# One of three stages: where the feed-forward weights are brought on chip

## The chip, the cores and the metric

The program runs on one core of a Trainium2 chip. The metric is the device time of one execution in microseconds (us). TensorE is called PE, VectorE DVE, ScalarE ACT, GpSimd POOL, and SyncE, which issues all the DMAs of this kernel, SP.

## What is computed

The reference, cut to what matters:

```python
x = x + attention(cond(x, lang, W1, b1, W2, b2, gamma, beta), Wq, Wk, Wv, Wf, bf)   # cond: adapter + layer norm
y = cond2(x, expert, fc1_w, fc1_b, fc2_w, fc2_b, experts_w, experts_b)
    # h = gelu(x @ fc1_w.T + fc1_b); 192 outputs by the shared fc2_w, 64 by the expert of the batch element
def ffn(y):                                   # every weight is ternary (-1, 0, 1) with a scale for each output
    h = silu(tlin(y, w1_w, w1_s)) * tlin(y, w2_w, w2_s)     # tlin(x, w, s) = (x @ w.T) * s
    h = gelu(tlin(h, h1_w, h1_s))
    h = gelu(tlin(h, h2_w, h2_s))
    return tlin(h, w3_w, w3_s)
out = x + ffn(y)                              # x: (16, 256, 256) float32, hidden width 1024
```

## The kernel before

The 16 batch elements of 256 tokens go through three stages, one after the other, with the results of each kept in scratch tensors in the chip's memory.

**Attention stage.** A software pipeline over the batch elements: in one iteration `b`, PE does the adapter and the projections of element `b + 2`, a first pass of scores for the row maxima of `b + 1`, the scores proper of `b`, and the output products of `b - 1`. Twelve of these iterations are a loop of six pairs. The row maxima of an element become two more rows of its queries: ACT writes them to `m_t` (L518) and SP moves them with four small DMAs into `q_t` (`move_maxima`, L249 to L256), for which the first `scores` of that element waits (L943).

**Conditional stage** (L1110 to L1136). A loop over 8 tiles of 512 tokens. In each tile PE makes 8 units of the first layer (L1120, from `tile_hi` and `tile_lo`, the high and low part of the tile's input), then the shared output (L1127), then the output with the expert's columns (L1134). ACT applies the gelu into one of two buffers of `g_raw` (L567), and DVE splits each into `g_hi` and `g_lo` (L772, L774). After the eight splits of a tile, DVE splits the input of the next tile (`split_x`, L716 and L718), ors an eighth of the feed-forward weights into `bits` (`or_bits`, L756) and adds the biases into `y` (L792, L795). In the last tile the order differs: `or_bits` stands ahead of the eight splits, since the bits must be reduced by the end of the stage (L783 to L787); from them a flag is made that says whether the feed-forward may use its weights in one rounded pass. PE reads it and branches (L1195).

For each tile SP loads two experts (L327, L328; each needs a register loaded from memory first), and the next tile's input `tile_in` (L336), then waits until `y` is ready and stores it (L351). The next tile's loads come behind that wait. In the last tile the load of `tile_in` is that of the first input of the feed-forward (L349). POOL makes the high and low part of the expert's weights (L470, L473).

**Feed-forward stage** (L1165 to L1193). Again 8 tiles; PE multiplies with `ffn_w` (L1157), which lies on chip as a whole: 22,528 columns of float32 in 128 partitions, 11.5 MB.

How `ffn_w` gets there: the weights are first copied from the input to a scratch tensor (`store_ffn`, L263), a sixteenth (1,408 columns, `SHARE`) with each batch element of the attention stage, and from there loaded on chip (`load_ffn`, L267), also a sixteenth each time, behind a wait for its copy. Both are issued by SP in the attention stage. `CHECK` is an eighth, 2,816 columns. All DMAs go through one hardware queue, in the order in which SP issues them.

Of the kernel before, what the change touches and what calls it, by code (L numbers as in the profile page):

```python
# [17 lines left out]
B, T, D = 16, 256, 256  # L18
# [32 lines left out]
SHARE = FFN_COLS // B  # L51
CHECK = FFN_COLS // TILES
# [15 lines left out]
def build(nc, x_t, x_tok, lang, expert, cond_w1, cond_w2, cond_vec, w_qv, w_k, w_f, b_f, ident_d, mask_d, key_row_d,  # L68
          fc1_w, fc1_b, fc2_w, fc2_b, exp_w, exp_b, ffn_d, ffn_s, out_t):
    ctx = ExitStack()  # L70
    with ctx:
# [29 lines left out]
        s = {}  # L101
# [118 lines left out]
        def settle(eng, name):  # L220


            eng.sem_inc(s[name], 1)

        @block.sync
        def _(sp):
# [36 lines left out]
            def store_ffn(b):  # L263
                cols = bass.ds(b * SHARE, SHARE)
                sp.dma_start(ffn_scratch[:, cols], ffn_d[:, cols]).then_inc(s["ffn_copied"], 16)

            def load_ffn(b):  # L267
                cols = bass.ds(b * SHARE, SHARE)
                sp.wait_ge(s["ffn_copied"], 16 * (b + 1))
                settle(sp, "sp_settled")  # L270
                sp.dma_start(ffn_w[:, cols].bitcast(F32), ffn_scratch[:, cols]).then_inc(s["ffn_loaded"], 16)


            load_front(0)
            sp.dma_start(ident[:, :], ident_d).then_inc(s["const_loaded"], 16)
# [10 lines left out]
            load_front(1)  # L286
            load_front(2)
            store_ffn(0)
            load_ffn(0)
            move_maxima(0, 0)  # L290
            load_front(3)
            store_ffn(1)
            load_ffn(1)
            move_maxima(1, 1)
            with sp.Fori(0, (B - 4) // 2) as pair:
                for step in (1, 2):
                    b = 2 * pair + step
                    store_ffn(b + 1)
                    load_front(b + 3)
                    load_ffn(b + 1)  # L300
                    store_x1(b - 1)
                    load_resid(b)
                    move_maxima(b + 1, 1 - step % 2)
            sp.wait_ge(s["x1_stored"], HEAD + 16 * BT)
            sp.dma_start(xa[:, :, :], x1_scratch[:, :, 0:TW]).then_inc(s["xa_loaded"], 16)
            for b in range(B - 3, B + 1):
                if b < B - 1:
                    store_ffn(b + 1)
                    load_ffn(b + 1)
                store_x1(b - 1)  # L310
                if b < B:
                    load_resid(b)
                if b < B - 1:
                    move_maxima(b + 1, (b + 1) % 2)
                if b == B - 2:
                    sp.wait_ge(s["fc1_split"], 1)
                    sp.dma_start(fc1_raw[:, :], fc1_w[:, 1]).then_inc(s["raw_loaded"], 16)
            sp.wait_ge(s["x1_stored"], HEAD + 16 * B)
            sp.wait_ge(s["phase1_over"], 4)


            sp.dma_start(fc2_raw[:, :, :], fc2_w).then_inc(s["fc2_loaded"], 16)
# [15 lines left out]
            def cond2_tile(t, more):  # L338
                if not is_first(t):
                    sp.wait_ge(s["expert_split"], HEAD + BT * t)  # L340
                    sp.wait_ge(s["y_ready"], HEAD + (1 + BT) * t)
                    settle(sp, "sp_settled")
                load_expert(t)
                if more:
                    load_x(t + 1)
                else:
                    sp.wait_ge(s["xa_split"], HEAD + TILES)
                    sp.wait_ge(s["y_stored"], HEAD + 16)
                    sp.dma_start(yc[:, :, :], y_scratch[:, :, 0:TW]).then_inc(s["yc_loaded"], 16)  # L349
                sp.wait_ge(s["y_ready"], HEAD + (1 + BT) * (t + 1))  # L350
                sp.dma_start(y_scratch[:, :, bass.ds(t * TW, TW)], y[:, :, :]).then_inc(s["y_stored"], 16)  # L351
# [238 lines left out]
        def _(dve):  # L590
# [148 lines left out]
            dve.wait_ge(s["phase1_over"], 4)  # L739


            dve.wait_ge(s["ffn_loaded"], 16 * B)
            def split_y(t):
                dve.wait_ge(s["yc_loaded"], 16 * (t + 1))
                if is_first(t):
# [6 lines left out]

            def or_bits(t):

                dve.wait_ge(s["bits_step"], t + 1)
                nc.vector.tensor_tensor(bits[:, :], bits[:, :], ffn_w[:, bass.ds(t * CHECK, CHECK)].bitcast(U32), ALU.bitwise_or).then_inc(s["bits_step"], 1)  # L756

# [508 lines left out]
```

## Time and profile before

| | |
|---|---|
| median of 3 runs | 1232.09 us (1232.05 to 1235.82) |
| the profiled execution | 1232.09 us, its span 1230.4 us |
| attention stage | 0 to about 387 us of the span |
| conditional stage | about 387 to 573 us |
| feed-forward stage | about 579 us to the end |
| PE busy | 1179.1 us, 96% of the span |
| DVE busy | 692.0 us, 56% |
| DMA | 18.6% of 16 engines' span, 70.44 MB |

PE is busy nearly throughout, so what matters is what PE does and where it stands still. The profiled execution took what the median run took, so sums against it are sums against the median.

### The profile page before, as it was taken

The page shows a single profiled execution, that of the slowest core. Times are in us where ns is not written, and L with a number is a line of the kernel's source. Part 1 is how long each engine was busy: PE and PEld are TensorE (multiplying, and loading weights), DVE is VectorE, ACT ScalarE, POOL GpSimd, SP SyncE. Part 2 cuts the span into 40 slices and gives each one's busy share as a digit, 9 for nine tenths or more (in the row PEclk, how much of TensorE's full clock was granted, in tenths as well). Part 3 has the DMA queues.
Part 4 walks back from the last instruction along what each step waited for, and adds up shares of the span by engine and source line. Part 5 has one row for each costly group of instructions (what it writes and reads, how often), then busy time and mean ns, then how long its engine had stood idle before and what let it go on. Part 6 is the DMA issues. An engine that isn't in the chain of part 4 may idle for free.

```text
span 1230.4 us, 19224 instructions
## 1 busy us (share of the span) xinstructions
PE 1179.1 (96%) x6404; PEld 942.4 (77%) x6434; DVE 692.0 (56%) x1264; ACT 400.4 (33%) x649; POOL 171.8 (14%) x235
## 2 busy tenths in 40 slices
PE   4899999999988899997999999999999999999998
PEld 3577777777756788886888888888888888888886
DVE  2867767676754887886535335335353263443532
ACT  1456465555643323222212213122122131221221
POOL 1233333334332211311000000000000000000000
PEclk9999999999999899998999999999999999999999
DMA  3343444444432212222001001010010010100100
GB/s 97 114 132 112 130 123 125 124 128 122 135 101 67 71 51 77 76 68 87 1 1 52 0 0 51 0 51 0 0 51 0 0 51 0 51 0 0 34 0 17
DMA packets 45417, 70.76 MB, mean 58 GB/s; under 512 B 12096, under 2 KB 26320, under 8 KB 45392
## 3 DMA queue, kind: packets, MB, share of 16 engines
q1 hardware_dynamic: 45392, 70.44, 18.6%
q8 instruction: 14, 0.23, 0.1%
q14 instruction: 11, 0.09, 0.0%
HBM read 57.32 MB, written 24.12 MB: 66 GB/s over the span
## 4 chain that ended last, share of the span: by engine, by line
PE 88%; DVE 6%; issue 2%; DMA 1%; SPq 1%; ACT 1%; POOL 1%; DVEq 0%; POOLq 0%; ACTq 0%
PE bank L1157 53%; PE bank L1120 6%; PE bank L1134 3%; PE bank L949 3%; PE bank L930 3%; PE bank L1127 3%; PE bank L970 2%; PE bank L1007 2%; DVE neg_max L640 2%; PE bank L912 2%; PE bank L896 2%; PE bank L933 1%; PE bank L885 1%; PE bank L870 1%; PE bank L862 1%
## 5 line engine op out<-in xcount | busy, mean ns | idle before, releaser
L1157 PE MATMUL bank<-h_lo,ffn_w 128*128 128x512 f32 x1152 | 450.8, 391 | 0.0
L1157 PE MATMUL bank<-h_hi,ffn_w 128*128 128x512 f32 x1152 | 450.8, 391 | 0.0
L1157 PEld LDWEIGHTS bank<-h_lo,ffn_w 128*128 128x128 f32 x1152 | 216.4, 188 | 47.3
L1157 PEld LDWEIGHTS bank<-h_hi,ffn_w 128*128 128x128 f32 x1152 | 216.3, 188 | 47.3
L819 DVE CAST h_hi<-h_raw 128x512 fp32r<-128x512 f32 x192 | 82.1, 427 | 300.3 <-ACT h_raw L587 298.1
L587 ACT ACTIVATE h_raw<-bank,scales 128x512 f32<-128x512 f32 x128 | 87.2, 687 | 322.0 <-PE bank L1157 321.9
L640 DVE TENSOR_REDUCE neg_max<-bank 128x2 f32<-128x512 f32 (+1 forms) x192 | 126.1, 686 | 53.0 <-remote 42.1
L821 DVE TENSOR_TENSOR h_lo<-h_raw,h_hi 128x512 fp32r<-128x512 f32 x192 | 133.0, 693 | 6.6
L501 ACT ACTIVATE p<-bank 128x512 f32<-128x512 f32 x192 | 111.3, 598 | 68.8 <-PE bank L949 65.2
L1157 PE MATMUL bank<-tile_hi,ffn_w 128*128 128x512 f32 x256 | 101.5, 397 | 7.0 <-issue 7.0
L1157 PE MATMUL bank<-tile_lo,ffn_w 128*128 128x512 f32 x256 | 101.3, 396 | 0.0
L949 PE MATMUL bank<-q_t,keys 128*128 128x512 f32 x192 | 94.8, 511 | 4.6 <-DMA q_t<-m_t 4.1
L930 PE MATMUL bank<-keys,q_t 128*128 128x256 f32 (+1 forms) x256 | 85.6, 390 | 7.3 <-DVE neg_max L640 6.4
L429 POOL TENSOR_SCALAR_AFFINE_SELECT p<-p 128x512 f32<-128x512 f32 (+1 forms) x96 | 75.7, 789 | 72.8 <-ACT p L501 72.8
L930 PEld LDWEIGHTS bank<-keys,q_t 128*128 128x128 f32 x256 | 47.8, 190 | 20.1 <-DVE neg_max L640 10.7
L829 DVE SCALAR_TENSOR_TENSOR h_raw<-bank,scales,sil 128x512 f32<-128x512 f32 x64 | 47.8, 746 | 27.0 <-ACT sil L580 27.0
L1157 PEld LDWEIGHTS bank<-tile_hi,ffn_w 128*128 128x128 f32 x256 | 48.9, 191 | 17.9 <-issue 7.1
L580 ACT ACTIVATE sil<-bank,scales 128x512 f32<-128x512 f32 x64 | 43.3, 688 | 55.7 <-PE bank L1157 54.4
L1157 PEld LDWEIGHTS bank<-tile_lo,ffn_w 128*128 128x128 f32 x256 | 48.8, 191 | 10.7
L774 DVE TENSOR_TENSOR g_lo<-g_raw,g_hi 128x512 fp32r<-128x512 f32 x64 | 54.4, 849 | 2.2
L567 ACT ACTIVATE g_raw<-bank,fc_bias 128x512 f32<-128x512 f32 x64 | 43.3, 690 | 34.8 <-DVE g_lo L774 17.9
L949 PEld LDWEIGHTS bank<-q_t,keys 128*128 128x128 f32 x192 | 37.6, 197 | 16.6 <-ACT p L501 7.8
(110 smaller groups left out, 1494.3 us busy)
## 6 DMA issues: line engine op xcount, KB each, us to landing
ffn_scratch<-in_ffn_d SPq DMA_DIRECT2D x16, 704.0 KB, 4.5
ffn_w<-ffn_scratch SPq DMA_DIRECT2D x16, 704.0 KB, 4.1
xt<-in_x_t SPq DMA_DIRECT2D x16, 256.0 KB
xtok<-in_x_tok SPq DMA_DIRECT2D x16, 256.0 KB
resid<-in_x_t SPq DMA_DIRECT2D x16, 256.0 KB, 3.1
x_scratch<-x SPq DMA_DIRECT2D x16, 256.0 KB, 2.6
tile_in<-x_scratch SPq DMA_DIRECT2D x8, 512.0 KB, 4.1
exp_raw<-in_exp_w SPq DMA_DIRECT2D x16, 256.0 KB, 2.7
```

The lines of the kernel that those rows point to most:

```text
L429: nc.gpsimd.affine_select(out=v, in_=v, compare_op=ALU.is_ge, fill=0.0, base=0, pattern=[[0, v.shape[1]], [1, P]], channel_multiplier=-1). ...
L501: nc.scalar.activation(dst.rearrange("p c t -> p (c t)"), score_bank[par][:, :], ACT.Exp).then_inc(s["exp_done"], 1)
L587: nc.scalar.activation(h_raw[:, m % 2, :], banks[g % 8][:, :], ACT.Gelu, scale=sc[:, m:m + 1]).then_inc(s["c_act"], 1)
L640: nc.vector.tensor_reduce(neg_max[:, t, first:first + pairs, :].rearrange("p c a -> p (c a)"), max_bank[u % 2][:, :].rearrange("p (c k) -> ...
L774: nc.vector.tensor_tensor(g_lo[:, m, :], g_raw[:, m % 2, :], g_hi[:, m, :].bitcast(F32), ALU.subtract).then_inc(s["act_ready"], 1)
L819: nc.vector.tensor_copy(dst_hi, src).then_inc(s["c_hi"], 1)
L821: nc.vector.tensor_tensor(dst_lo, src, dst_hi.bitcast(F32), ALU.subtract).then_inc(s["c_ready"], 1)
L829: nc.vector.scalar_tensor_tensor(out=h_raw[:, m % 2, :], in0=banks[(2 * m + 1) % 8][:, :], scalar=SC_W2[:, m:m + 1], in1=sil[:, m % 2, :], ...
L930: mm(dst[:, 2 * c * seen:2 * (c + 1) * seen].rearrange("p (a k) -> p a k", a=2), q_t[odd][:, first + c, t * P:(t + 1) * P], keys[odd][:, : ...
L949: mm(score_bank[par][:, :].rearrange("p (c t) -> p c t", c=pairs), keys[odd][:, par, k0:k0 + P], q_t[odd][:, first:first + pairs, q0:T], s ...
L1120: last = mm(banks[m % 6][:, :], w[:, k, cols], v[:, k, :], start=i == 0, stop=i == len(passes) - 1)
L1157: last = mm(bank, w_at(at, k, width, m), v_at(v, k), start=k == 0 and i == 0, stop=k == tiles - 1 and i == 1)
```

## The change

The load of the feed-forward weights is taken out of the attention stage, where it stood behind the wait for the copy. The copies stay. SP now issues one load of an eighth (1,408 KB instead of 704 KB) in each tile of the conditional stage, behind the two experts' loads and ahead of the load of `tile_in`. SP waits once, at the end of the attention stage, until all copies have landed. DVE, which waited at the beginning of the conditional stage for all 16 loads, now waits in each `or_bits(t)` for load `t`.

```diff
--- before.py
+++ after.py
@@ -264,12 +264,9 @@
                 cols = bass.ds(b * SHARE, SHARE)
                 sp.dma_start(ffn_scratch[:, cols], ffn_d[:, cols]).then_inc(s["ffn_copied"], 16)
 
-            def load_ffn(b):
-                cols = bass.ds(b * SHARE, SHARE)
-                sp.wait_ge(s["ffn_copied"], 16 * (b + 1))
-                settle(sp, "sp_settled")
+            def load_ffn(t):
+                cols = bass.ds(t * CHECK, CHECK)
                 sp.dma_start(ffn_w[:, cols].bitcast(F32), ffn_scratch[:, cols]).then_inc(s["ffn_loaded"], 16)
-
 
             load_front(0)
             sp.dma_start(ident[:, :], ident_d).then_inc(s["const_loaded"], 16)
@@ -286,18 +283,15 @@
             load_front(1)
             load_front(2)
             store_ffn(0)
-            load_ffn(0)
             move_maxima(0, 0)
             load_front(3)
             store_ffn(1)
-            load_ffn(1)
             move_maxima(1, 1)
             with sp.Fori(0, (B - 4) // 2) as pair:
                 for step in (1, 2):
                     b = 2 * pair + step
                     store_ffn(b + 1)
                     load_front(b + 3)
-                    load_ffn(b + 1)
                     store_x1(b - 1)
                     load_resid(b)
                     move_maxima(b + 1, 1 - step % 2)
@@ -306,7 +300,6 @@
             for b in range(B - 3, B + 1):
                 if b < B - 1:
                     store_ffn(b + 1)
-                    load_ffn(b + 1)
                 store_x1(b - 1)
                 if b < B:
                     load_resid(b)
@@ -317,6 +310,7 @@
                     sp.dma_start(fc1_raw[:, :], fc1_w[:, 1]).then_inc(s["raw_loaded"], 16)
             sp.wait_ge(s["x1_stored"], HEAD + 16 * B)
             sp.wait_ge(s["phase1_over"], 4)
+            sp.wait_ge(s["ffn_copied"], 16 * B)
 
 
             sp.dma_start(fc2_raw[:, :, :], fc2_w).then_inc(s["fc2_loaded"], 16)
@@ -341,6 +335,7 @@
                     sp.wait_ge(s["y_ready"], HEAD + (1 + BT) * t)
                     settle(sp, "sp_settled")
                 load_expert(t)
+                load_ffn(t)
                 if more:
                     load_x(t + 1)
                 else:
@@ -739,7 +734,6 @@
             dve.wait_ge(s["phase1_over"], 4)
 
 
-            dve.wait_ge(s["ffn_loaded"], 16 * B)
             def split_y(t):
                 dve.wait_ge(s["yc_loaded"], 16 * (t + 1))
                 if is_first(t):
@@ -752,6 +746,7 @@
 
             def or_bits(t):
 
+                dve.wait_ge(s["ffn_loaded"], 16 * (t + 1))
                 dve.wait_ge(s["bits_step"], t + 1)
                 nc.vector.tensor_tensor(bits[:, :], bits[:, :], ffn_w[:, bass.ds(t * CHECK, CHECK)].bitcast(U32), ALU.bitwise_or).then_inc(s["bits_step"], 1)
```

The order on SP around the first move of maxima (names are those of the tensors, destination first; ISA and REGISTER rows work out addresses). Before:

```order
L265 DMA ffn_scratch<-in_ffn_d 128x1408
L271 DMA ffn_w<-ffn_scratch 128x1408 [waits ffn_copied]
L256 DMA q_t<-m_t 1x8x256 [waits max_t_out]
L256 DMA q_t<-m_t 1x8x256 x3
L229 TENSOR_LOAD in_lang_ptr
```

With the change:

```order
L265 DMA ffn_scratch<-in_ffn_d 128x1408
L256 DMA q_t<-m_t 1x8x256 [waits max_t_out]
L256 DMA q_t<-m_t 1x8x256 x3
L229 TENSOR_LOAD in_lang_ptr
L229 REGISTER_ALU
```

The load and its wait no longer stand between the copy and the moves of maxima.

SP in a tile of the conditional stage, from the second expert on. Before:

```order
L327 DMA exp_raw<-in_exp_w 128x512
L328 ISA
L328 DMA fc_bias<-in_exp_b 64x1
L335 REGISTER_ALU
L336 ISA [waits xa_split]
L336 DMA tile_in<-x_scratch 128x2x512
L350 ISA
L351 ISA [waits y_ready]
L351 DMA y_scratch<-y 256x1x512
```

With the change:

```order
L321 DMA exp_raw<-in_exp_w 128x512
L322 ISA
L322 DMA fc_bias<-in_exp_b 64x1
L269 ISA
L269 DMA ffn_w<-ffn_scratch 128x2816
L329 REGISTER_ALU
L330 ISA [waits xa_split]
L330 DMA tile_in<-x_scratch 128x2x512
L345 ISA
L346 ISA [waits y_ready]
L346 DMA y_scratch<-y 256x1x512
```

The load of an eighth stands in front of the load of the next tile's input.

DVE at the beginning of the last tile. Before:

```order
L806 COMPARE_AND_BRANCH
L756 TENSOR_TENSOR bits<-bits,ffn_w 128x2816 [waits bits_step]
L772 CAST g_hi<-g_raw 128x512 [waits raw_ready]
L774 TENSOR_TENSOR g_lo<-g_raw,g_hi 128x512 [waits hi_ready]
L772 CAST g_hi<-g_raw 128x512 [waits raw_ready]
```

With the change:

```order
L801 COMPARE_AND_BRANCH
L751 TENSOR_TENSOR bits<-bits,ffn_w 128x2816 [waits bits_step,ffn_loaded]
L767 CAST g_hi<-g_raw 128x512 [waits raw_ready]
L769 TENSOR_TENSOR g_lo<-g_raw,g_hi 128x512 [waits hi_ready]
L767 CAST g_hi<-g_raw 128x512 [waits raw_ready]
```

The order is the same; the `or_bits` in front of the splits now also waits for a load.

## Rows read from the trace of the kernel before

**Rows 1.** Windows: length, busy us of PE PEld DVE ACT POOL, clock, DMA share, GB/s

```profile
231.60:253.10 21.50, 21.12 (x166) 15.70 (x167) 15.62 (x38) 12.10 (x23) 8.08 (x12) 1.00 0.42 126
316.00:338.00 22.00, 21.62 (x168) 15.98 (x169) 16.19 (x38) 12.31 (x24) 8.08 (x12) 1.00 0.52 160
528.00:550.00 22.00, 22.00 (x121) 19.18 (x120) 17.53 (x23) 6.70 (x9) 4.95 (x4) 1.00 0.23 72
```

**Rows 2.** Chain of work that ended last, conditional stage: start us, us, what

```profile
538.74 5.44 PE bank L1127 x24
544.18 5.75 PE bank L1134 x48
549.94 9.56 PE bank L1120 x42
...
573.40 5.80 issue
```

**Rows 3.** Timeline, 41 to 48 us: start us, us, engine, line, work [idle before <-releaser]

```profile
41.99 0.37 ACT L518 ACTIVATE m_t<-bank 32x256 fp32r<-32x256 f32 x1 [4.87 <-PE bank L938]
...
42.82 0.36 SPq L271 DMA_DIRECT2D ffn_w<-ffn_scratch  x1
...
43.29 2.88 SPq L256 DMA_DIRECT2D q_t<-m_t  x4
...
47.77 0.50 PE L949 MATMUL bank<-q_t,keys 128*128 128x512 f32 x1 [1.36 <-DMA q_t<-m_t]
```

**Rows 4.** Timeline of SP, seventh and last tile of the conditional stage

```profile
536.74 0.59 SPq L336 DMA_DIRECT2D tile_in<-x_scratch  x1
551.01 0.65 SPq L351 DMA_DIRECT2D y_scratch<-y  x1
...
558.09 0.61 SPq L349 DMA_DIRECT2D tile_in<-y_scratch  x1
```

**Rows 5.** DMA issues: form, count, KB each, median us from issue to landing

```profile
ffn_w<-ffn_scratch SPq DMA_DIRECT2D x16, 704.0 KB, 4.1
...
tile_in<-x_scratch SPq DMA_DIRECT2D x8, 512.0 KB, 4.1
```

**Rows 6.** The line of the load, L271: spread of its landings

```profile
DMA to landing us min/median/max: 3.9/4.1/5.3
```

**Rows 7.** Windows, the first microseconds of the feed-forward stage

```profile
578.00:580.00 2.00, 0.80 (x2) 0.72 (x3) 0.00 (x0) 0.00 (x0) 0.00 (x0) 0.50 0.43 116
580.00:582.00 2.00, 2.00 (x6) 1.51 (x6) 0.00 (x0) 0.63 (x1) 0.00 (x0) 0.50 1.01 354
```

**Rows 8.** Timeline of DVE, end of the seventh tile

```profile
542.03 1.77 DVE L716 CAST tile_hi<-tile_in 128x1024 fp32r<-128x1024 f32 x1
...
547.98 0.75 DVE L792 TENSOR_SCALAR y<-bank,fc_bias 128x512 f32<-128x512 f32 x1
549.97 0.88 DVE L795 TENSOR_SCALAR y<-bank,fc_bias 128x256 f32<-128x256 f32 x2 [1.24 <-PE bank L1134]
```

**Rows 9.** Timeline of DVE, last tile

```profile
550.77 3.08 DVE L756 TENSOR_TENSOR bits<-bits,ffn_w 128x2816 uint32<-128x2816 uint32 x1
553.77 0.42 DVE L772 CAST g_hi<-g_raw 128x512 fp32r<-128x512 f32 x1
554.22 0.69 DVE L774 TENSOR_TENSOR g_lo<-g_raw,g_hi 128x512 fp32r<-128x512 f32 x1
...
559.09 0.42 DVE L772 CAST g_hi<-g_raw 128x512 fp32r<-128x512 f32 x1
...
563.47 1.66 DVE L774 TENSOR_TENSOR g_lo<-g_raw,g_hi 128x512 fp32r<-128x512 f32 x1
565.05 0.68 DVE L749 CAST tile_hi<-tile_in 128x1024 fp32r<-128x1024 f32 x1
...
572.47 0.86 DVE L795 TENSOR_SCALAR y<-bank,fc_bias 128x256 f32<-128x256 f32 x2
```

**Rows 10.** Timeline of POOL, last tile

```profile
561.54 3.04 POOL L473 TENSOR_TENSOR fc2b_lo<-exp_raw,fc2b_hi 128x512 fp32r<-128x512 f32 x2
```

## The prediction

> **What bounds the kernel now.** I read the windows of the stages first, to see where PE has time to give back. In the attention stage PE is busy 21.12 of 21.50 us of one iteration, and 21.62 of 22.00 in a stretch with more DMA traffic: in both 0.38 us idle at full clock. In a tile of the conditional stage it is busy 22.00 of 22.00 us [rows 1]. So in the loops of both stages PE is the limit, and a transfer matters only where PE or its feeder waits for it. Then the chain of waits: it runs along PE through the tiles, but behind the last first-layer units (549.94 + 9.56 = 559.50) it leaves PE and runs along DVE up to 573.4, where 5.8 us follow in which the stages change over [rows 2]. DVE in the last tile is busy without a hole from 550.77 to 573.3 [rows 9]. That is the place to watch: what delays DVE there delays the end by the same amount. Last, the timelines of SP and DVE, for who issues a load when, and who needs it.
>
> **Part 1: the load and its wait leave the attention stage.** In the loop nothing waits for them: the 0.38 us are PE's own. I take 0. The bound on the gain is that all idle goes, 0.38 x 13 iterations = 4.9 us; since a stretch at 160 GB/s has the same idle time as one at 126 [rows 1], I stay at 0.
>
> At the first move of maxima there is a gain. SP waits there for the copy, issues the load at 42.82 and the moves from 43.29 on; but ACT has `m_t` ready at 41.99 + 0.37 = 42.36 [rows 3]. Without the load the moves go out at about 42.4, 0.9 us earlier. PE had waited 1.36 us for them at 47.77 [rows 3], so it can use all of it: **-0.9** (bounds 0, if another engine is late next, and -1.4, PE's whole wait). What is late next is PE's own work before, which ends at 47.77 - 1.36 = 46.4.
>
> At the stage's end SP waits for the last copy, which was issued with element 15 some 40 us before: 0.
>
> **Part 2: seven tiles of the conditional stage.** The load of an eighth takes the place in SP's order of the load of `tile_in`, which was issued at 536.74 and landed 4.1 us later, at 540.8; DVE came to it at 542.03 [rows 4, 5, 8]. The queue works the loads off in order, so the landing of `tile_in` moves back. A sixteenth (704 KB) lands in 4.1 us [rows 5]. The rate of the fullest stretch is 354 GB/s [rows 7]; another 704 KB at it are 2.04 us, so the eighth lands 6.1 us after its issue, and the 512 KB of `tile_in` behind it take 1.48 us more: 7.6, at 544.3.
>
> What can the chain bear? From DVE's start on `tile_in` to its first `y` are 547.98 - 542.03 = 5.95 us, in which the cast took 1.77 us; undisturbed it takes 0.68 [rows 8, 9], so 4.86 us. The second `y` waits for PE until 549.97, and the first takes 0.75 [rows 8]. So `tile_in` may land at 549.97 - 0.75 - 4.86 = 544.4 at the latest. My estimate is 544.3: **it just fits, term 0**. PE itself needs the split only at 549.94 [rows 2] and has slack (544.3 + 1.9). But SP issues the next tile's loads only when `y` is ready. So beyond 544.4, each tenth is paid again in each of the six tiles before the last: the chain load, split, `or_bits`, `y` would be the limit and not PE. Bounds: the landing lies between 542.9 (the eighth and `tile_in` move side by side: 4.1 + 2.04) and 545.5 (the slowest landing of a sixteenth, 5.3 [rows 6], + 2.04 + 1.48). Above 544.4 that is 1.1 us a tile: 0 to +6.6.
>
> The Trainium skill, "DMA: Bandwidth & Descriptors", section on the anatomy of one DMA, fits a transfer as 2.0 us plus its bytes at 436 GB/s; by that, an estimate, eighth and `tile_in` together land after 6.5 us instead of 7.6, and the fit would leave a spare of about a microsecond. The same page's bandwidth section gives about 358 GB/s for memory-side transfers, and our 354 agrees [rows 7].
>
> **Part 3: the last tile.** Here `or_bits` stands ahead of the splits, and the eighth it needs is issued only after SP has stored the `y` of the tile before (551.01) and fetched two experts: at 558.09, where the load of `tile_in` stood [rows 4]. It lands at 558.1 + 6.1 = 564.2. DVE would have begun at 550.77 [rows 9] and now stands for 13.4 us, with all eight splits and everything to the stage's end queued behind. Not all of it is lost. Before, the splits took 565.05 - 553.77 = 11.28 us, since the last ones were slowed (1.66 us against 0.69) [rows 9] while POOL worked on the experts' weights up to 564.6 [rows 10]. Now POOL is done before they begin, and they run at the pitch of the first ones, (559.09 - 553.77) / 5 = 1.064 us, so 8.5 us [rows 9]. `or_bits` from 564.2, splits from 567.2 (3.0 us as before, 550.77 to 553.77), done at 575.7 instead of 565.05: **+10.6**. From there DVE's way to the second `y` is 7.4 us as before (565.05 to 572.47), so it starts at 583.1.
>
> Does PE cover or add anything? It has finished its first-layer units (they need only two gelus, which no split holds up) and stands from 560.7 to 568. Its shared output follows the splits (5.44 / 8 = 0.68 us for each against a pitch of 1.06), ends at 576.4, and the experts' output ends 5.75 us later [rows 2], at 582.2, 0.9 before DVE wants it. Nothing is added at full clock.
>
> Bounds: the eighth lands like a sixteenth (4.1) and the term is 8.6; it takes 5.3 + 2.04 = 7.3 and the term is 11.9; if in addition the splits run as slowly as before, 14.7.
>
> **Sum.** -0.9 + 0 + 10.6 = +9.7 on the profiled execution of 1232.1 us, which is also the median: **1241.8 us**.
>
> **Rivals.**
>
> *A. The tiles become bound by the loads.* Same mechanism as in part 2, with a landing past 544.4. At 1.1 us in each of six tiles the time is 1241.8 + 6.6 = 1248.4; half of that, 1245.1, is as likely. For it: my estimate leaves 0.1 us. Against: DVE and SP had nothing that late before. Chance 0.22.
>
> *B. A cold PE in the last tile.* PE stands for over 7 us there. After the pause of at least 5.8 us at the stage's end [rows 2] the granted clock was 0.50 when it came back [rows 7], that is 1.2 instead of 2.4 GHz. At half clock all through, the experts' output takes 11.5 us, ends at 587.9, and the end is 4.8 later: 1246.6. Against it: PE has 8 us of fairly dense work between, which should bring the clock back before. The Trainium skill, "TensorE: Matmul & The Clock Gate", section on HAM oscillation, names pauses for a DMA between bursts as what sends the clock down, and counts the time at half clock as half lost; if only the shared output is hit, nothing is lost here, since DVE sets its pace. Chance 0.06.
>
> *C. The attention loop gives back its idle time* (4.9 us): 1236.9. The same idle at different traffic [rows 1] speaks against it. Chance 0.05.
>
> *D. The traffic slows the engines in the attention stage,* not by waits but in the instructions themselves, and without 704 KB of writes in each iteration they run shorter. From 9.7 / 13 = 0.75 us in an iteration of 21.5 this decides, and at 1.1 us (5%) the time is 1241.8 - 14.3 = 1227.5, faster. Against it: two iterations whose traffic differs by a quarter have the same PE time. The Trainium skill, "SBUF — State Buffer", section on the bandwidth pool, says contention there is a matter of locked ports and not of a shared total, which excludes D. Chance 0.03.
>
> *E. The wait is shorter than I think,* for instance since SP reaches the eighth earlier. For no measurable change (within 0.3%, 3.7 us, about what a measurement of this kernel can tell) it must land before 558.2, when by its rows it is just being issued [rows 4]. Chance 0.03.
>
> **How the numbers follow.** The forecast has 0.61. Its own bounds are 1239.3 (parts at -1.4, 0, 8.6) to 1244.0 (0, 0, 11.9). The range takes it in with most of A and B: 1239.0 to 1249.0, leaving out C, D, E and the far end of A. Slower by over 0.3%: forecast, A, B and most of C, 0.92. Within: E and a rest of C, 0.05. Faster: D, 0.03.
>
> **What the new profile would show.** The chain of waits should have a DMA of `ffn_w` in the last tile, and DVE's `or_bits` there a wait of some 13 us that such a landing ended, with the first split at about 566 (all 0.9 earlier than above). PE should be idle some 7 us behind its last first-layer units. POOL should be done before the splits, and these be even at 1.06 us. PE in the middle tiles should stay at 22.0 of 22.0 us with a pitch of 22.1; a pitch of 22.5 or more, with DVE waiting for `tile_in`, is rival A. Iterations of the attention stage should keep their 21.5 us, and the first scores come 0.9 us earlier. I am wrong in kind if DVE does not wait in the last tile, or if the attention iterations get shorter by more than 0.3 us.

## The result and the profile after

| | before | with the change |
|---|---|---|
| median (20 runs each) | 1234.58 us (1230.87 to 1249.10) | 1244.83 us (1242.13 to 1257.58) |
| the profiled execution | 1232.09 us | 1247.21 us |
| its span | 1230.4 us | 1245.5 us |
| first scores / first store of `y` / last store of `y` | 47.77 / 418.30 / 573.36 | 46.56 / 418.99 / 588.20 |

The time is 1.0075 times that of before, with an interval of 1.0053 to 1.0097, that is 6.5 to 12.0 us more. The forecast was 1241.8 us and +9.7. The profiled executions lie 2.5 us below the median of their kernel (before) and 2.4 above it (after), so their spans, 15.1 us apart, show too much. Where they differ for another reason than the change is said below. Three of the 20 executions before and one of the 20 after took 13 to 15 us more than the median of the rest; without these four the medians are 1233.70 and 1244.73 us, 11.0 apart.

The page of the changed kernel: the engines' busy time, and their shares of the chain that ended last.

```profile
PE 1185.8 (95%) x6404; PEld 945.8 (76%) x6434; DVE 675.7 (54%) x1264; ACT 400.6 (32%) x649; POOL 169.0 (14%) x235
...
PE 75%; DVE 9%; DMA 5%; SPq 5%; issue 4%; ACT 1%; POOL 0%; DVEq 0%; POOLq 0%; ACTq 0%
```

A PE busy for 95% of the span still looks like the only limit. But DMA and SP's queue hold a tenth of the chain. Where they enter it, the chain shows (rows from the seventh tile on; start us, us, what):

```profile
540.24 0.43 SPq L269
540.97 6.95 DMA tile_in<-x_scratch
548.03 0.70 DVE tile_hi L711
...
549.90 2.52 DVE bits L751
...
554.61 0.66 SPq L346
...
561.65 6.70 DMA ffn_w<-ffn_scratch
568.38 3.09 DVE bits L751
571.47 0.35 DVE g_hi L767
...
586.64 0.75 DVE y L787
...
588.24 5.80 issue
594.04 16.05 PE bank L1152 x59
```

Before, this stretch ran along PE up to 559.50 and then along DVE [rows 2]. Now it goes round through the loads. The landing of `tile_in` releases DVE's split, `or_bits` and `y` follow, then SP's store, and behind the store the next loads. In the last tile the link is the landing of the eighth.

DVE at the same two places (start us, us, engine, line, work, idle before and what ended it):

```profile
548.03 0.69 DVE L711 CAST tile_hi<-tile_in 128x1024 fp32r<-128x1024 f32 x1 [5.42 <-DMA tile_in<-x_scratch]
...
568.38 3.09 DVE L751 TENSOR_TENSOR bits<-bits,ffn_w 128x2816 uint32<-128x2816 uint32 x1 [13.94 <-DMA ffn_w<-ffn_scratch]
571.39 0.42 DVE L767 CAST g_hi<-g_raw 128x512 fp32r<-128x512 f32 x1
571.84 0.69 DVE L769 TENSOR_TENSOR g_lo<-g_raw,g_hi 128x512 fp32r<-128x512 f32 x1
...
579.89 0.69 DVE L743 CAST tile_hi<-tile_in 128x1024 fp32r<-128x1024 f32 x1
```

The wait of 13.94 us answers to an `or_bits` that began without one at 550.77 [rows 9]. The eight splits behind it take 579.89 - 571.39 = 8.50 us. They took 11.28 when POOL's work lay beside them [rows 9, 10].

SP in the seventh and the last tile (start us, us, engine, line, work), against [rows 4]:

```profile
540.24 0.43 SPq L269 DMA_DIRECT2D ffn_w<-ffn_scratch  x1
540.97 0.60 SPq L330 DMA_DIRECT2D tile_in<-x_scratch  x1
554.61 0.66 SPq L346 DMA_DIRECT2D y_scratch<-y  x1
...
561.65 0.59 SPq L269 DMA_DIRECT2D ffn_w<-ffn_scratch  x1
```

The landings (form, count, KB each, median us from issue to landing), against 4.1 us for 704 KB and 4.1 us for 512 KB in [rows 5]:

```profile
ffn_w<-ffn_scratch SPq DMA_DIRECT2D x8, 1408.0 KB, 6.4
...
tile_in<-x_scratch SPq DMA_DIRECT2D x8, 512.0 KB, 7.0
```

At the start, two pieces of the chain and PE's first scores, against 43.29 and the 1.36 us of [rows 3]:

```profile
42.37 0.79 SPq L256
...
44.59 1.93 DMA q_t<-m_t
...
46.56 0.50 PE L944 MATMUL bank<-q_t,keys 128*128 128x512 f32 x1 [0.24 <-DMA q_t<-m_t]
```

**Where the time went, by stretches of the profiled executions.** The eight stores of `y` cut the conditional stage into pieces that don't depend on a choice of mine.

| stretch | before | after | difference |
|---|---|---|---|
| to the first scores | 47.77 | 46.56 | -1.21 |
| from there to the first store of `y` | 370.53 | 372.43 | +1.90 |
| six tiles, first to seventh store | 132.71 | 135.62 | +2.91 |
| last tile, seventh to eighth store | 22.35 | 33.59 | +11.24 |
| last store to the end of the span | 657.0 | 657.3 | +0.3 |

Through nearly all of the attention stage the second row stays near zero: from the second to the 14th element the changed kernel begins its scores 1.17 to 1.30 us earlier. With the 15th the lead falls to 0.49 us, and with the 16th it is 0.95. The 1.90 us are lost at that stage's end and in the first tile. There the granted clock is at its lower level, 1.2 GHz, for different lengths in different executions. Windows on PE of the kernel before (length, PE busy, clock, DMA share, GB/s):

```profile
360.00:370.00 10.00, 6.18 (x74) 0.93 0.34 109
370.00:380.00 10.00, 8.73 (x91) 0.90 0.16 47
403.00:418.00 15.00, 12.13 (x63) 0.77 0.00 0
```

and with the change:

```profile
360.00:370.00 10.00, 6.46 (x74) 0.84 0.36 108
370.00:380.00 10.00, 9.24 (x88) 0.82 0.16 49
403.00:418.00 15.00, 11.70 (x59) 0.77 0.21 81
```

The experiments suggest that this is chance and not the change. Ten executions were profiled in which the early move of maxima has no load ahead of it. Their first store of `y` came at 415.81 to 419.30, mean 417.96. Four with the load ahead of it: 418.30 to 420.55, mean 419.12. The means differ by 1.2 us, the size of the gain at the first scores. But the ten alone spread over 3.5 us, so the two means don't prove it.

### The profile page after: what moved, and what is told of

Its sections match the earlier page's. It is cut to its first block, busy times and chain, and to the rows that moved or that the text cites. A ratio compares the mean times of both kernels' runs of the same rounds, so it can differ in the third digit from the quotient of the medians.

```text
span 1245.5 us, 19192 instructions
## 1 busy us (share of the span) xinstructions
PE 1185.8 (95%) x6404; PEld 945.8 (76%) x6434; DVE 675.7 (54%) x1264; ACT 400.6 (32%) x649; POOL 169.0 (14%) x235
## 4 chain that ended last, share of the span: by engine, by line
PE 75%; DVE 9%; DMA 5%; SPq 5%; issue 4%; ACT 1%; POOL 0%; DVEq 0%; POOLq 0%; ACTq 0%
PE bank L1152 52%; PE bank L944 3%; DMA tile_in<-x_scratch 3%; PE bank L925 3%; PE bank L1002 2%; DVE neg_max L635 2%; PE bank L965 2%; PE bank L907 2%; SPq L320 2%; PE bank L891 2%; DVE bits L751 1%; PE bank L928 1%; PE bank L880 1%; PE bank L865 1%; PE bank L857 1%
## 5 line engine op out<-in xcount | busy, mean ns | idle before, releaser
L1152 PEld LDWEIGHTS bank<-tile_lo,ffn_w 128*128 128x128 f32 x256 | 48.9, 191 | 10.8
L944 PEld LDWEIGHTS bank<-q_t,keys 128*128 128x128 f32 x192 | 38.0, 199 | 15.9 <-ACT p L496 7.9
L928 PE MATMUL bank<-mask,ident_b 128*128 128x256 bf16 (+1 forms) x162 | 49.5, 305 | 0.0
```

The lines of the kernel that those rows point to most:

```text
L928: mm(diag, ident_b[:, :], mask[:, 0:2 * pairs, :], start=False, stop=True).then_inc(s["max_mm"], 1)
L944: mm(score_bank[par][:, :].rearrange("p (c t) -> p c t", c=pairs), keys[odd][:, par, k0:k0 + P], q_t[odd][:, first:first + pairs, q0:T], s ...
L1152: last = mm(bank, w_at(at, k, width, m), v_at(v, k), start=k == 0 and i == 0, stop=k == tiles - 1 and i == 1)
```

## The experiments

The runs came in three sets of four, in the order in which they stand here. Each set has its own runs of the kernel before: medians 1233.92, 1234.23 and 1233.48 us. Every ratio is against those of its set. Line numbers in rows are those of each kernel. Diffs are against the changed kernel unless they say otherwise.

**One tile early.** In tile `t` the eighth of tile `t + 1` is loaded, and eighth 0 at the end of the attention stage.

```diff
+                    sp.wait_ge(s["ffn_copied"], 32)
+                    load_ffn(0)
             sp.wait_ge(s["x1_stored"], HEAD + 16 * B)
...
                 load_expert(t)
-                load_ffn(t)
                 if more:
+                    load_ffn(t + 1)
                     load_x(t + 1)
```

> The changed kernel, but each eighth is loaded one tile earlier (the first at the end of the attention stage), so the last tile issues no load. Theory (the last tile's wait costs most, the lateness of tile_in the rest): the wait of 13.9 us on DVE in the last tile goes and the last tile is 11.2 us shorter, while the middle tiles stay at a pitch of 22.6 us: about 1244.8 - 11.2 = 1233.6. Rival (the middle tiles are most of the loss, the wait is mostly covered): the last tile gets less than 4 us shorter and the time stays over 1240.

Measured: 1234.47 us, ratio 1.0011 (0.9975 to 1.0047). The last tile takes 22.34 us as before, and no wait for `ffn_w` is left: the loss is in the last tile's wait. My expectation for the middle tiles missed. Their pitch is (552.00 - 419.23) / 6 = 22.13 us, though DVE still waits 3.48 us for `tile_in` in the seventh. The landing is just early enough here. Yet `tile_in` stands behind a whole eighth as with the change. From the issue of the eighth both had landed after 7.34 to 7.41 us in five of the six tiles, where the change needed 7.72 to 8.24. Why the same two loads land sooner here stays open.

**The input first.** `tile_in` goes ahead of the eighth of the same tile.

```diff
                 load_expert(t)
-                load_ffn(t)
                 if more:
                     load_x(t + 1)
...
+                load_ffn(t)
                 sp.wait_ge(s["y_ready"], HEAD + (1 + BT) * (t + 1))
```

> The changed kernel, but SP issues the load of tile_in ahead of the eighth. Theory: tile_in lands some 4 us after its issue again, the middle tiles go back to a pitch of 22.1 us (six tiles, -3.1 us), and the last eighth lands 1.5 us later, since the 512 KB are in front of it: about 1244.8 - 3.1 + 1.5 = 1243.2. Rival (the middle tiles are late because of the wait for the eighth in or_bits, not because of tile_in): the pitch stays at 22.6 and the time rises to about 1246.

Measured: 1245.53 us, ratio 1.0109 (1.0063 to 1.0155). The pitch of the middle tiles is back at (548.72 - 415.81) / 6 = 22.15, so it was the place behind the eighth that made `tile_in` late. The last tile pays: `or_bits` waits 15.28 us and the tile takes 34.95. By the profiles that is some 2.7 us gained and 1.4 lost; the timing can't tell this kernel from the changed one.

**Both.** `tile_in` first, then the eighth of the next tile; eighth 0 at the end of the attention stage, as in the one-tile-early run.

```diff
                 load_expert(t)
-                load_ffn(t)
                 if more:
                     load_x(t + 1)
+                    load_ffn(t + 1)
```

> One tile early and behind tile_in. Theory: both losses go, and the 1.2 us that the first move of maxima gained stay: about 1234.6 - 1.2 = 1233.4, pitch 22.1 us, no wait in the last tile. Rival (the loads in the conditional stage cost by their traffic, wherever they stand): 1237 or more.

Measured: 1231.43 us, ratio 0.9977 (0.9944 to 1.0011). Its windows hold no loss: pitch (550.64 - 417.57) / 6 = 22.18, last tile 22.33, first scores at 46.65. Its chain runs from tile to tile along PE alone, as in [rows 2]:

```profile
499.96 5.16 PE bank L1131 x43
505.12 10.91 PE bank L1117 x48
516.03 5.44 PE bank L1124 x24
521.47 5.86 PE bank L1131 x48
527.33 10.91 PE bank L1117 x48
```

It has seven of the change's eight loads in the conditional stage (eighth 0 is issued at 364.8), and its ratio is 0.9977 where the change has 1.0075, some 12 us less. Against the kernel before it is 2.5 us faster by the medians, but the interval holds 1.

**The check behind the splits.** The last tile's `or_bits` moves behind the splits and behind `split_y`.

```diff
             def cond2_tile(t, more):
-                if not more:
-                    or_bits(t)
                 for m in range(KH):
...
                     split_y(0)
+                    or_bits(t)
```

> The changed kernel, but in the last tile the or of the last eighth stands behind the eight splits and the split of the next input, so the splits do not queue behind the wait. Theory: the eighth lands at 568.3 in the profile of the changed kernel, the splits end at about 567.5 and the split of the input at 569.4, so DVE never stands for the load; the second y starts about 9 us earlier: about 1235.5. Rival (what costs is the landing itself, whatever stands behind it): the time stays within 3 us of 1244.8.

Measured: 1239.70 us, ratio 1.0056 (1.0023 to 1.0089). The wait for the eighth is gone and the last tile falls from 33.59 to 26.56 us, but not to the value expected. DVE in that tile:

```profile
564.96 0.98 DVE L767 TENSOR_TENSOR g_lo<-g_raw,g_hi 128x512 fp32r<-128x512 f32 x1
570.16 0.69 DVE L743 CAST tile_hi<-tile_in 128x1024 fp32r<-128x1024 f32 x1 [4.22 <-DMA tile_in<-y_scratch]
```

The expected 1235.5 missed: I had overlooked that the feed-forward's first input is queued behind the same eighth. Once `or_bits` no longer hides it, its landing is the next wait, 4.22 us.

**The changed kernel again.** No edit.

> The changed kernel once more, for a second profile. Theory: the pitch of the middle tiles is again 22.4 us or more and DVE waits there for tile_in, DVE waits about 13.5 us in the last tile; which stretches run at half clock differs. Rival (the 22.6 us of the first profile were a chance of that execution): pitch 22.2 or less.

Measured: 1246.09 us, ratio 1.0121 (1.0077 to 1.0165). The profile repeats the pieces: pitch (552.93 - 416.82) / 6 = 22.69, last tile 33.19 with a wait of 13.53, and first scores at 46.60.

**Half the bytes.** A sixteenth of each pair is loaded in the attention stage behind its copy, as before, and the other in its tile.

```diff
             def load_ffn(t):
-                cols = bass.ds(t * CHECK, CHECK)
+                cols = bass.ds(t * CHECK + SHARE, SHARE)
...
             store_ffn(0)
+            load_half(0)
             move_maxima(0, 0)
```

> The changed kernel, but half of each eighth (a sixteenth, 704 KB) is loaded in the attention stage behind its copy, as before the change, and the other half in the tile. Theory (the bytes in front of tile_in and of the last check cost): tile_in lands some 2.3 us earlier than with the eighth, so the middle tiles are bound by PE again at 22.1 us (-3), and the wait in the last tile shrinks by 2.3 us; the 1.2 us at the first move of maxima are gone again. About 1244.8 - 3 - 2.3 + 1.2 = 1240.7. If SP's register loads are late in the loop by some 0.35 us also here, that lateness comes from the added instructions in the loop and not from the bytes.

Measured: 1244.34 us, ratio 1.0108 (1.0057 to 1.0160). Of the pieces, these went about as expected: the pitch is (553.24 - 420.55) / 6 = 22.12, the last wait is 12.11 us, 1.83 less than 13.94 where 2.3 was expected, and the first scores are back at 47.94. The first store of `y` came 1.6 us later than with the change, and the last tile, 32.41, is only 1.2 shorter, since its `or_bits` took 3.73 us instead of 3.09. Its profile alone would give 1243.3 - 1245.5 = -2.2 us of span, where the medians show -0.5, and -1.8 against the 1246.09 of the changed kernel in the same set. The expected 1240.7 missed. Halving the bytes removes a small part of the loss, at a size that these six runs can't tell from none.

**Twice the bytes.** Each tile loads two eighths, of which the second is the next tile's; weights are so loaded twice.

```diff
+                cols = bass.ds(0 if isinstance(t, int) else (t + 1) * CHECK, CHECK)
+                sp.dma_start(ffn_w[:, cols].bitcast(F32), ffn_scratch[:, cols]).then_inc(s["ffn_loaded"], 16)
...
-                dve.wait_ge(s["ffn_loaded"], 16 * (t + 1))
+                dve.wait_ge(s["ffn_loaded"], 32 * (t + 1))
```

> The changed kernel, but each tile loads two eighths (the second again in its own tile, the last time the first eighth), and each or waits for both. 1408 KB more in front of tile_in. Theory: tile_in lands 1441792 bytes / 354 GB/s = 4.1 us later plus 0.4 us of issue, which the chain of load, split, or and y passes on in full: pitch about 22.6 + 4.5 = 27.1 us in six tiles, and 4.5 us more in the last: about 1244.8 + 31.5 = 1276. Rival (PE is the limit of the middle tiles and the load is covered): pitch under 23 and the time about 1250.

Measured: 1269.33 us, ratio 1.0279 (1.0247 to 1.0311), less than the 1276 expected. The pitch is (574.22 - 419.30) / 6 = 25.82, 3.2 us over that of the change, and the last wait 16.70. So the tiles of this kernel are bound by the loads, as rival A has it, and each further microsecond of landing is paid in each tile. DVE in the sixth tile:

```profile
541.72 0.69 DVE L713 CAST tile_hi<-tile_in 128x1024 fp32r<-128x1024 f32 x1 [10.58 <-DMA tile_in<-x_scratch]
542.44 1.23 DVE L715 TENSOR_TENSOR tile_lo<-tile_in,tile_hi 128x1024 fp32r<-128x1024 f32 x1
543.59 3.08 DVE L753 TENSOR_TENSOR bits<-bits,ffn_w 128x2816 uint32<-128x2816 uint32 x1
```

The split begins 19.2 us after the store of `y` (522.49), and with the change 15.9 in the seventh tile (548.03 - 532.13); the means over six tiles are 19.3 and 16.0. The second eighth cost 3.3 us and not the 4.1 that 354 GB/s [rows 7] give: 1,408 KB in 3.3 us are 437 GB/s. A window (length, busy us of PE PEld DVE ACT POOL, clock, DMA share, GB/s) shows it directly:

```profile
534.00:538.00 4.00, 2.62 (x20) 2.19 (x19) 0.00 (x0) 0.00 (x0) 1.91 (x2) 1.00 1.04 439
```

**The last eighth first.** In the last tile the eighth goes ahead of the two experts.

```diff
+                if not more:
+                    load_ffn(t)
                 load_expert(t)
                 if more:
+                    load_ffn(t)
                     load_x(t + 1)
```

> The changed kernel, but in the last tile SP issues the eighth ahead of the two experts. Theory: it is issued about 0.7 us behind the store of y instead of 7.0, so the wait in the last tile ends some 6.3 us earlier; POOL's work on the experts falls into the splits again and costs up to 2.8 us of that: 1244.8 - 6.3 + (0 to 2.8), about 1240. Rival (SP's issue isn't what makes the eighth late): less than 2 us gained.

Measured: 1243.03 us, ratio 1.0077 (1.0050 to 1.0105); that is 3.1 us less than the changed kernel in the same set, where 3.5 to 6.3 were expected. The eighth is issued 0.97 us after the store of `y` instead of 7.04, and the wait falls by 5.4 us. Half of that is lost again (last tile 30.89 us, 2.7 less), since now the experts come late and POOL's work lies beside the splits once more. DVE in that tile:

```profile
560.21 3.09 DVE L753 TENSOR_TENSOR bits<-bits,ffn_w 128x2816 uint32<-128x2816 uint32 x1 [8.51 <-DMA ffn_w<-ffn_scratch]
...
564.99 1.50 DVE L769 CAST g_hi<-g_raw 128x512 fp32r<-128x512 f32 x1
566.52 1.63 DVE L771 TENSOR_TENSOR g_lo<-g_raw,g_hi 128x512 fp32r<-128x512 f32 x1
```

The splits take 574.45 - 563.22 = 11.2 us here, against 8.5 with the change. That is the saving which part 3 of the prediction had counted, with its sign turned.

**The kernel before again.** No edit to the kernel before.

> The kernel before once more, for a second profile and for what two timings of one kernel differ by. The sum of the changed kernel's parts against the first profile of before (13.5 to 15.1 us) is larger than the difference of the medians (10.3 and 11.9). If the first profile was a lucky one, PE's places in this one are 1 to 3 us later by the end, above all at the stage changes, where stretches at half clock differ; if not, they agree within 0.5 us and the rest of the gap stays open. Ratio to before: 1.000.

Measured: 1234.76 us, ratio 1.0022 (0.9993 to 1.0052). Two timings of one kernel thus differ by 0.2%, 2.7 us. Its pitch and last tile are 22.1 and 22.34 us, as in the first profile. Its first scores come at 48.48, 0.7 us later than there, after a wait of 2.15 us for the same moves, and its last store of `y` at 573.89, 0.5 us later. So the gain at the first scores is 1.2 to 1.9 us, by which profile of before it is measured.

**The moves first.** Against the kernel before: the first move of maxima goes ahead of the first load.

```diff
             store_ffn(0)
-            load_ffn(0)
             move_maxima(0, 0)
+            load_ffn(0)
```

> The kernel before with one change: SP issues the four moves of the first maxima ahead of the first load of weights and its wait. Theory: all of the change's gain in the attention stage is this place: the first scores come 1.1 to 1.2 us earlier and stay so through the twelve iterations, time 1.1 us less or lost in the spread. Rival (the gain needs the loads gone from the loop): PE is back at its old places within the loop.

Measured: 1231.61 us, ratio 0.9988 (0.9966 to 1.0011). PE:

```profile
46.54 0.50 PE L949 MATMUL bank<-q_t,keys 128*128 128x512 f32 x1 [0.24 <-DMA q_t<-m_t]
```

The first scores come at 46.54, as with the change. So the gain at the start is one of order, and is to be had without moving any load out of the stage. That it reaches the end of the program agrees with the medians, but the interval holds 1.

**A small load in the tile.** Against the kernel before: everything stays, and SP loads 4 columns (2 KB) in each tile at the place of the eighth, for which `or_bits` waits. SP also waits once for all 16 loads before the conditional stage.

```diff
                 load_expert(t)
+                cols = bass.ds(t * CHECK, 4)
+                sp.dma_start(ffn_w[:, cols].bitcast(F32), ffn_scratch[:, cols]).then_inc(s["bit_loaded"], 16)
...
+                dve.wait_ge(s["bit_loaded"], 16 * (t + 1))
                 dve.wait_ge(s["bits_step"], t + 1)
```

> The kernel before with one more DMA of 2 KB (four columns of ffn_w, again) in each tile of the conditional stage, where the changed kernel has its eighth, and a wait for it in the or of the tile. It tells apart why SP issues the first expert's load 3.5 to 4.0 us behind the store of y in the loop instead of 3.2 to 3.4. If the added instructions in the loop do it, it is at 3.6 also here; if the bytes in flight, at 3.3. Time as before, ratio within 0.002, pitch 22.1 us: 2 KB don't delay tile_in.

Measured: 1243.01 us, ratio 1.0074 (1.0042 to 1.0106), where a ratio within 0.002 was expected. I had meant it to price the instructions alone and had not thought of the last tile. It is the clearest run of the study. SP issues the load there 7.55 us after the store of `y`; it lands 1.9 us later, and DVE stands:

```profile
560.78 3.16 DVE L760 TENSOR_TENSOR bits<-bits,ffn_w 128x2816 uint32<-128x2816 uint32 x1 [9.64 <-DMA ffn_w<-ffn_scratch]
563.86 0.83 DVE L776 CAST g_hi<-g_raw 128x512 fp32r<-128x512 f32 x1
564.73 1.63 DVE L778 TENSOR_TENSOR g_lo<-g_raw,g_hi 128x512 fp32r<-128x512 f32 x1
```

The last tile takes 31.81 us, 9.5 more than before, for 2 KB. Of the change's wait of 13.94 us, some 9.6 are the place in SP's order, with the 1.9 us in which even 2 KB land, and some 4.3 are the bytes. The split is rough, since SP issued the load 0.5 us later here than with the change. The middle tiles stay at (551.30 - 418.67) / 6 = 22.1.

**Input, experts, next eighth.** A try at something better still, with eighth 0 at the end of the attention stage as before.

```diff
-                load_expert(t)
-                load_ffn(t)
                 if more:
                     load_x(t + 1)
+                load_expert(t)
+                if more:
+                    load_ffn(t + 1)
```

> As the kernel with both repairs (one tile early, behind tile_in), but SP issues tile_in ahead of the experts too, so that it lands long before DVE wants it. Theory: the pitch is 22.1 in all middle tiles (instead of 22.1 to 22.2), the last tile has no wait, the start gain of 1.1 us stays: about 1231 against 1234.3. The experts come 0.8 us later; POOL is done some 0.8 us later, and PE wants them only behind the shared output. Rival: POOL's later work falls on other DVE instructions and gives back up to 1 us a tile.

Measured: 1261.11 us, ratio 1.0222 (1.0171 to 1.0273), where about 1231 was expected: a plain miss. Its six runs lie between 1250.80 and 1268.79 us, and the profiled one, 1251.50, is near the lowest. So what the profile shows explains about 18 us of the loss, and what made the other runs longer stays open. The first expert's load is issued 5.6 us after the store of `y` (424.37 - 418.73) instead of 3.6. POOL starts later and lies beside DVE's tile split and `or_bits`. POOL in two tiles:

```profile
433.27 5.20 POOL L471 TENSOR_TENSOR fc2b_lo<-exp_raw,fc2b_hi 128x512 fp32r<-128x512 f32 x2
...
460.46 6.21 POOL L471 TENSOR_TENSOR fc2b_lo<-exp_raw,fc2b_hi 128x512 fp32r<-128x512 f32 x2
```

against 3.04 us in [rows 10]. PE's waits (total us, times, longest):

```profile
PE bank L1132 <- POOL fc2b_lo L471: 14.1, 6, 4.5
```

PE stops in six tiles. Behind the first two stops its granted clock also falls: 0.84 and 0.87 in the windows 435 to 440 and 440 to 447, 0.57 and 0.79 in 465 to 470 and 470 to 476. The stores of `y` are 28.3, 29.3 and then 23.6 to 23.8 us apart; the last tile has its 22.3.

## Why the prediction was right, and where not

**The attention stage, term -0.9: right, measured -1.2.** The moves went out at 42.37 instead of 43.29, 0.9 us earlier as said. The other 0.3 us the term didn't have: the last move landed 1.93 us after its issue (44.59 to 46.52), and before, with the load ahead of it in the queue, 2.19 us (45.53 to 47.72). PE's wait shrank from 1.36 to 0.24 us, and nothing else took its place. The moves-first run gives the same with the load kept, so it was the load's place ahead of the moves. In the profile of after this gain is hidden by the 1.90 us of clock and stage end; the ten-against-four comparison agrees with it, without proving it. Rivals C and D are out: the gap between the kernels is -1.17 to -1.30 us through the whole loop, so its iterations kept their length with 704 KB of writes fewer in each. The Trainium skill, "SBUF — State Buffer", in its section on the bandwidth pool, says that transfers and engines don't share a total; the trace agrees.

**The middle tiles, term 0: this step failed.** The text said "it just fits", with a landing at 544.3 against a limit of 544.4. Its terms added up without rounding give 544.36 for both, so the sum had no spare at all, and the 0.1 us counted against rival A was rounding. Counted from the store of `y`, the limit was 544.4 - 528.92 = 15.5 us; measured were 15.9 in the seventh tile. Two sizes were off in that tile. SP issued the eighth 8.1 us after the store (540.24 - 532.13) where `tile_in` had been at 7.8 (536.74 - 528.92): the first expert's load is already later by that. And the two landings together took 7.8 us (548.03 - 540.24) where I had 7.6. That is rival A at half of its size, since the pitch rose by 0.48 us (after) and 0.57 (again) and not by 1.1: +2.9 and +3.4 us. The size varies: two more kernels keep the change's order in these tiles, and there the pitch was (555.04 - 419.26) / 6 = 22.63 in the check-behind run, but only (551.87 - 417.70) / 6 = 22.36 in the last-eighth-first run, +3.1 and +1.5 us. PE's windows hardly betray it (22.25 of 22.50 us busy in the seventh tile), since PE's next first-layer units had slack: they begin at 552.17 in the last tile, 2.2 us after 549.94 [rows 2], while the store of `y` slipped by 3.6 (554.61 - 551.01). What counts is the store, for the last eighth is queued behind it. The input-first, both and half-the-bytes runs each take the landing back under the limit, and the pitch with it; twice the bytes raises it by 3.2.

Why SP's first load of a tile comes 0.3 to 0.4 us later in kernels with an eighth in the loop stays open. The small load adds the same instruction, and there that load is issued 3.2 to 3.4 us after the store as before and the middle tiles kept their 22.1 us, so it is not the instruction alone. Nor is it bound to an eighth: in the second profile of before one tile in six has it at 3.65, and with half the bytes two in six at 3.7.

**The last tile, term +10.6: right, measured +11.2 and +10.8.** All links are in the rows. The eighth was issued 7.04 us after the store of `y` (estimate 7.08), and took 6.7 us where I had 6.1. The splits then ran at 1.06 us each as said, since POOL was done. PE stood 9.4 us and not the 7 of the text: the store of `y`, behind which the eighth is queued, had slipped 1.4 us further than PE's own work, and the landing took 0.6 longer.

```profile
572.68 0.77 PE L1122 MATMUL bank<-g_hi,fc2a_hi 128*128 128x512 f32 x1 [9.44 <-DVE g_lo L769]
```

The landing is the term's error. The Trainium skill, "DMA: Bandwidth & Descriptors", section on the anatomy of one DMA, has 2.0 us and 436 GB/s, an estimate of 5.3 us for an eighth. It gives this fit for DMAs that GpSimd issues, which the prediction didn't say; all loads here are SP's, and the median landing was 6.4. For 2 KB, though, its fixed part fits the 1.9 us seen here, and its rate fits the 437 GB/s of a second eighth.

Rival B, the cold PE, came and cost nothing. The clock was at the lower level for most of 568 to 579 us:

```profile
568.00:579.00 11.00, 6.32 (x16) 0.53 0.04 17
579.00:588.00 9.00, 8.00 (x60) 1.00 0.00 0
```

There PE follows DVE's splits. At 1.2 GHz it needs 1.28 us for the three products of a split (573.24 to 574.52, and again to 575.80), and the splits come every 1.06 us, so it fell behind, but only by a little. It was back at 2.4 GHz for the experts' output, which began at 580.97 and, at 5.75 us as before [rows 2], ended at 586.7, 0.6 before DVE wanted it at 587.31. Rival E would have needed the landing at 558.2; it came at 568.4.

**The sum.** By the profiles the parts are -1.2, +2.9 to +3.4 and +10.8 to +11.2, together +13. The medians say +10.3 (+9.3 by the ratio, 6.5 to 12.0) and, in the second timing, +11.9 (+14.9 by the ratio, 9.5 to 20.4). That +9.7 lies so near the +10.3 is in part luck: the middle term that the forecast lacks, some 3 us, is about as large as the gap between the parts and the medians. The forecast's 3.0 us below the measured time come mostly from the base: 1232.09 was the low side of a kernel whose 20 runs have their median at 1234.58. One to three microseconds between the parts and the medians stay unexplained. Two timings of the kernel before differ by 2.7 us in ratio, so that much is within what this measurement leaves open.

A gain from a lighter attention stage was never there to be had: nothing in that loop waited for the loads. The change's one real gain, 1.2 us, is a matter of order. The cost is mostly one of order too: with the eighths one tile ahead and behind `tile_in`, and so only the first of them still in the attention stage, the same loads cost nothing measurable.

## What to carry to other kernels

When a load is moved next to its user, price its place in the issuing queue before its bytes: list what the queue does between the event that frees it and the load, for the loop's ordinary turn and for the last one, where the order of the consumer may differ. A loop in which a store waits for the result and the next loads stand behind that store has a pitch of its own, and where the sum leaves no spare the likeliest value of such a term is not zero. Issue loads one turn ahead of their use and behind those that are needed sooner, and look at who else is moved by that.

## What the hardware showed that I had not expected

- A load of 2 KB made the last tile 9.5 us longer, nearly as much as one of 1,408 KB (11.2).
- The second of two 1,408 KB loads in a row cost 3.3 us, 437 GB/s, and a 4 us window shows 439 GB/s, where the fullest stretch of the trace before had 354 [rows 7]. With a single eighth, too, a window of the changed kernel (564 to 566) has 417. The Trainium skill, "DMA: Bandwidth & Descriptors", section on bandwidth, gives about 358 GB/s as what binds transfers from memory, and also 425 GB/s as measured for 16 MB with one core streaming; these kernels, on one core, agree with the second. The prediction took its 354 as agreeing with the first, but it was no limit.
- DVE and POOL slow each other: `g_lo` takes 1.63 us instead of 0.69 beside POOL, and POOL's `fc2b_lo` 5.20 and 6.21 instead of 3.04 beside DVE. The Trainium skill, "SBUF — State Buffer", section on who interferes with whom, says that such pairs lock each other out for a whole instruction. That both engines were slowed where their work overlaps fits; that one stands for a whole instruction of the other, no row here shows. So where POOL's work lies decides 2.7 us of the last tile, and in the last experiment 14 us of PE's waits.
- The feed-forward's matmuls with `h_lo` took 391 ns on average in the first profile of before and 397 in the second, at a granted clock of 1.00 in both (650 to 1100 us). From the last store of `y` to the end that execution took 13 us more, so the granted clock alone does not say how long a matmul takes.
- With the same order at the start, the first store of `y` came anywhere from 415.8 to 419.3 us, at least in part by how long the clock stayed at its lower level at the attention stage's end and in the first tile. One pair of profiles can't show a microsecond there.
